# Half-array mask and memory-update matmuls, a reordered prob transpose and resets on ScalarE in a compressive-memory attention block

## What is computed

```
scores  = q @ k.T / 8, masked above the diagonal
att_dot = softmax(scores) @ v
sq, sk  = elu(q) + 1, elu(k) + 1
att_mem = (sq @ M) / (sq @ Z.T)
M, Z    = M + sk.T @ v, Z + sum(sk)          # starts again from memory0, z0 for each sequence
att     = gate * att_mem + (1 - gate) * att_dot
out     = att @ Wo
```

## Time and profile before

| | us |
|---|---|
| median of 3 runs | 1129.81 |
| lowest, highest | 1127.05, 1130.29 |
| the profiled execution, its own time | 1129.79 |
| its span from first to last instruction | 1128.0 |
| attention part (16 steps), about | from 42 to 905 in the span |
| one step in the steady state | 54.4 |

### The profile page before, as it was taken

The page is one execution under the profiler, slowest core; times in us unless marked ns, Lnnn a source line. Parts: engine busy times, 40 slices in busy tenths (PEclk is TensorE's granted clock), DMA queues, the critical chain, the costliest instruction groups (busy, mean ns, idle before and its releaser), DMA issues.

```text
span 1128.0 us, 18928 instructions
## 1 busy us (share of the span) xinstructions
PE 1026.4 (91%) x7108; PEld 726.0 (64%) x7172; DVE 779.3 (69%) x1514; ACT 617.2 (55%) x1259; POOL 561.9 (50%) x685
## 2 busy tenths in 40 slices
PE   2899999999999999899999999999998889999961
PEld 1577777776777777677777776777776755433431
DVE  4868686878778686969686968696857423434465
ACT  4556565445656464456565645565654444666562
POOL 3456565445656563547474635565654322222366
PEclk9999999999999999999999999999999889999985
DMA  5200000000000000000000000000000103000015
GB/s 159 48 11 10 14 7 16 5 20 1 20 1 20 1 20 2 19 1 20 1 20 1 20 10 10 10 11 10 1 11 1 32 0 159 1 0 0 1 38 112
DMA packets 14984, 23.82 MB, mean 21 GB/s; under 512 B 5424, under 2 KB 7216, under 8 KB 14384
## 3 DMA queue, kind: packets, MB, share of 16 engines
q1 hardware_dynamic: 13964, 19.36, 6.0%
q10 hardware_dynamic: 932, 3.28, 0.9%
HBM read 13.97 MB, written 8.65 MB: 20 GB/s over the span
## 4 chain that ended last, share of the span: by engine, by line
PE 76%; ACT 10%; DVE 8%; issue 2%; POOL 2%; DMA 1%; ACTq 0%; POOLq 0%; DVEq 0%
PE ps L1133 20%; PE ps L1230 11%; PE ps L1190 7%; PE ps L1342 7%; ACT arena L607 6%; PE ps L1177 4%; PE ps L1166 4%; PE ps L1196 4%; PE ps L1149 4%; PE ps L1355 3%; PE ps L1215 3%; PE ps L1202 3%; PE ps L1161 2%; DVE arena L855 2%; ACT arena L613 2%
## 5 line engine op out<-in xcount | busy, mean ns | idle before, releaser
L1133 PE MATMUL ps<-arena 128*128 128x512 f16 x1152 | 266.2, 381 | 6.7 <-DVE arena L807 5.2
L607 ACT ACTIVATE arena<-ps,arena 128x128 f32<-128x128 f32 x512 | 138.9, 382 | 126.7 <-DVE arena L855 126.7
L1133 PEld LDWEIGHTS ps<-arena 128*128 128x128 f16 x1152 | 112.9, 98 | 124.6 <-DVE arena L807 5.6
L830 DVE STREAM_TRANSPOSE arena<-ps 128x1024 f32<-128x1024 f32 x96 | 146.1, 1522 | 23.1 <-PE ps L1133 20.7
L436 POOL TENSOR_TENSOR arena<-arena 128x256 f32<-128x256 f32 x128 | 93.3, 729 | 136.2 <-DVE arena L874 69.5
L1190 PE MATMUL ps<-arena 128*128 128x65 f32 x1024 | 136.7, 277 | 10.3 <-ACT arena L613 4.7
L1190 PEld LDWEIGHTS ps<-arena 128*128 128x128 f32 x1024 | 128.4, 194 | 23.5 <-ACT arena L613 7.9
L421 POOL TENSOR_TENSOR arena<-arena 128x512 f32<-128x512 f32 x48 | 73.2, 1524 | 102.8 <-ACT arena L600 102.8
L782 DVE BATCH_NORM_STATS2 arena<-arena 128x6 f32<-128x256 f32 x100 | 36.9, 410 | 126.5 <-ACT arena L625 121.9
L1230 PE MATMUL ps<-arena 128*128 128x256 f32 x544 | 121.9, 382 | 0.3 <-ACT arena L619 0.3
L1230 PEld LDWEIGHTS ps<-arena 128*128 128x128 f32 x544 | 102.0, 190 | 16.1 <-ACT arena L619 1.4
(11 more groups left out here) (110 smaller groups left out, 1819.2 us busy)
## 6 DMA issues: line engine op xcount, KB each, us to landing
x_rows<-arena SPq DMA_DIRECT2D x17, 256.0 KB, 2.0
arena<-x_rows SPq DMA_DIRECT2D x4, 1024.0 KB, 7.9
out_dram<-arena SPq DMA_DIRECT2D x32, 128.0 KB, 2.9
arena<-in_L_attn_x_dram SPq DMA_DIRECT2D x62, 64.0 KB
arena<-in_L_attn_Wq_dram ACTq DMA_DIRECT2D x2, 512.0 KB, 12.2
arena<-in_L_attn_Wk_dram ACTq DMA_DIRECT2D x2, 512.0 KB, 15.2
arena<-in_L_attn_Wv_dram ACTq DMA_DIRECT2D x2, 512.0 KB, 17.8
arena<-in_L_attn_Wo_dram SPq DMA_DIRECT2D x8, 128.0 KB, 5.1
```

Of the source, the lines that this page charges most:

```text
L607: last = act.activation(Pr[:, par, j, :], s_bank[:, par, j * P:(j + 1) * P], ACT.Exp, bias=negm[:, par, j:j + 1])
L830: dve.transpose(dst[:, d0:d0 + 32], bank.rearrange("p w (d c) -> p d w c", c=C)).then_inc(x_free, 1)
L1133: last = pe.matmul(bank[:, w, :], xc[:, lx, k, w * P:(w + 1) * P], W16[lw][:, k, i, :], start=(n == 0), stop=(n == 5))
```

## The change

Six edits go together.

- **Mask.** Instead of two matmuls of 128 by 512, four: for each parity a 64-row identity (`ident2`) times `mask_top` into PSUM partitions 0 to 63 (512 columns), and times `mask_low` into partitions 64 to 127, there only the right 64 columns of each of the four blocks (256 columns). The left ones are first written by the score matmuls.
- **Update.** sk.T @ v is no longer computed in both halves of a group but only in `half == 1`, for all four `j`: eight matmuls of 128 rows by 64 output partitions and 65 columns instead of four of 128 by 130. VectorE adds it in `half == 1` alone, two adds of 64 x 260 in place of four of 64 x 130.
- **Order on TensorE.** In groups 0, 2 and 3 the turn of the next Q stands between the two parities' prob transposes, and K after them.
- **Copies of the probs.** `pt_full` counts parities, and ScalarE copies each parity's bank by itself (two of 128 x 512).
- **Resets** of M between sequence pairs: 48 VectorE copies of 64 x 130 become 24 ScalarE copies of 64 x 260, at four places of ScalarE's order, and TensorE waits for them in every segment 0.
- **Constants.** GpSimd builds only `identf` at the start, and the smaller mask and identity tiles after the low weights; TensorE waits for these before step 0.

```diff
@@ reset on ScalarE
-                def reset():
+                def reset(bp, s, g):
+                    if s != NSEG - 1 or bp == PAIRS - 1:
+                        return
+                    if bp >= 0:
+                        act.wait_ge(pm_full, bp * 32 + 8 * s + 2 * g + 2)
+                    for par in range(2):
+                        p = slice(64 * par, 64 * par + 64)
+                        act.activation(M[p, GP * g:GP * g + GP, par, :],
+                                       M0[p, GP * g % (H // 2):GP * g % (H // 2) + GP, :],
+                                       ACT.Copy).then_inc(m_reset, 1)
@@ take_p
-                    act.wait_ge(pt_full, bp * 16 + 4 * s + g + 1)
-                    act.activation(PT.rearrange("p h j i -> p (h j i)"), s_bank.rearrange("p h n -> p (h n)"),
-                                   ACT.Copy).then_inc(p_done, 1)
+                    for par in range(2):
+                        act.wait_ge(pt_full, bp * 32 + 8 * s + 2 * g + par + 1)
+                        last = act.activation(PT[:, par, :, :].rearrange("p j i -> p (j i)"), s_bank[:, par, :],
+                                              ACT.Copy)
+                    last.then_inc(p_done, 1)
@@ step on ScalarE
                     take_p(bp, s, 0)
+                    if s == 0 and bp > 0:
+                        reset(*before(bp, s), 3)
                     take_q(bp, s, 1)
@@ divide
-                    for par in range(2):
-                        p = slice(64 * par, 64 * par + 64)
-                        m = M[p, j:j + 2, par, :]
-                        if s < NSEG - 1:
-                            last = dve.tensor_tensor(m, T[p, :, par, :], m, ALU.add)
-                        elif bp < PAIRS - 1:
-                            last = dve.tensor_copy(m, M0[p, j0:j0 + 2, :])
+                    if half == 1 and s < NSEG - 1:
+                        new = pm_bank[:, :, 4 * DV1:6 * DV1].rearrange("p b (j e) -> p b j e", j=2)
+                        for par in range(2):
+                            p = slice(64 * par, 64 * par + 64)
+                            m = M[p, GP * g:GP * g + GP, par, :].rearrange("p (b j) e -> p b j e", b=2)
+                            last = dve.tensor_tensor(m, new[p], m, ALU.add)
                     last.then_inc(pm_free, 1)
@@ scores
-                        pe.matmul(s_bank[:, par, :], identb, maskS, start=True, stop=False)
+                        p = slice(64 * par, 64 * par + 64)
+                        pe.matmul(s_bank[0:64, par, :].rearrange("p (j i) -> p j i", j=GP), ident2[p],
+                                  mask_top[p].rearrange("p (a i) -> p a i", a=1).to_broadcast([64, GP, P]),
+                                  start=True, stop=False, skip_group_check=True)
+                    for par in range(2):
+                        p = slice(64 * par, 64 * par + 64)
+                        pe.matmul(s_bank[64:P, par, :].rearrange("p (j i) -> p j i", j=GP)[:, :, 64:P], ident2[p],
+                                  mask_low[p].rearrange("p (a i) -> p a i", a=1).to_broadcast([64, GP, 64]),
+                                  start=True, stop=False, skip_group_check=True)
@@ read_out
-                    if bp == 0 and s == 0:
-                        pe.wait_ge(m_reset, 2 * (g + 1))
+                    if s == 0:
+                        pe.wait_ge(m_reset, bp * 8 + 2 * (g + 1))
...
-                    if s < NSEG - 1:
+                    if half == 1 and s < NSEG - 1:
                         pe.wait_ge(sk_done, sk_count(bp, s, g) + 2)
-                        for a in range(2):
-                            h = GP * (g % 2) + 2 * half + a
-                            last = pe.matmul(pm_bank[:, a, 4 * DV1:6 * DV1],
-                                             sk[:, 2 * DK * (GP * (g - g % 2) + h):
-                                                2 * DK * (GP * (g - g % 2) + h + 1)], v[:, h, :, 0:DV1],
-                                             start=True, stop=True)
+                        for a in range(GP):
+                            h = GP * (g % 2) + a
+                            for par in range(2):
+                                unit = 2 * (GP * (g - g % 2) + h) + par
+                                last = pe.matmul(pm_bank[64 * par:64 * par + 64, a // 2,
+                                                         (4 + a % 2) * DV1:(5 + a % 2) * DV1],
+                                                 sk[:, DK * unit:DK * (unit + 1)], v[:, h, par, 0:DV1],
+                                                 start=True, stop=True)
@@ step on TensorE, group 2
-                    turn_probs(bp, s, 2)
-                    turn(bp, s, 3)
+                    turn_probs(bp, s, 2, 0)
+                    turn(bp, s, 3, "Q")
+                    turn_probs(bp, s, 2, 1)
+                    turn(bp, s, 3, "K")
```

More of the change, by code:

```diff
@@ L659, in step @@
                         take_q(bp, s, 0)
+                    reset(bp, s, 2)
                 act.sem_inc(p_done, 1)
                 take_q(0, -1, 0)
-                reset()
+                act.wait_ge(m_in, 64)
+                act.wait_ge(init, 1)
+                for g in range(GROUPS):
+                    reset(-1, NSEG - 1, g)
                 for bp, s in STEPS:
@@ L1167, in scores, with turn_probs @@
                                                  c[g % 2][p, j, :], start=False,
[L1168 removed]
+                                                 stop=(j == GP - 1 and n == 2), skip_group_check=True)
                     last.then_inc(s_full, 1)
[L1171 removed]
+                def turn_probs(bp, s, g, par):
                     G = 4 * s + g
[L1174 to L1177 removed]
+                    pe.wait_ge(e_done, bp * 32 + 2 * G + par + 1)
+                    for j in range(GP):
+                        last = pe.transpose(s_bank[:, par, j * P:(j + 1) * P], Pr[:, par, j, :], identf)
                     last.then_inc(pt_full, 1)
@@ L1276, in step @@
                     read_out(bp, s, 2, 1)
-                    turn_probs(bp, s, 3)
+                    turn_probs(bp, s, 3, 0)
                     if not last:
-                        turn(bp, s, 0)
+                        turn(bp, s, 0, "Q")
+                    turn_probs(bp, s, 3, 1)
+                    if not last:
+                        turn(bp, s, 0, "K")
                     read_out(bp, s, 3, 0)
```

59 lines of the change are left out of this document (29 added, 30 removed).

## The result

The changed kernel takes 1103.58 us (median of four runs, 1103.25 to 1103.98) against 1130.05 for the kernel before (1127.05 to 1130.38). The ratio is 0.977, with a 95% interval from 0.976 to 0.979. In the two profiled executions the span fell from 1128.0 to 1101.4 us, by 26.6 where 16.6 was expected.

The account below looks back on a forecast made before the run. TensorE was taken as mostly the bound, with VectorE's chains nearly full in C and D. Segments 1 and 2 -6.0, segment 0 -3.4, segment 3 -2.5, resets -4.7: -16.6 from 1129.81 gave 1113 us, range 1099 to 1124.

Parts of the forecast that it names:

- The central step: VectorE's chain to the next K sets C, so TensorE's saving there is lost: about 1.0 us of its gain.
- C: Stretch of a step between masks, 10.50 us before; VectorE busy 9.89; forecast +0.1 in segments 1 and 2.
- segments 1 and 2: Eight steps: A +0.1, B -0.45, C +0.1, D -0.5, sum -0.75 a step, -6.0 us in all.
- A: Stretch from group 0's mask to group 1's, 11.90 us before; chain through K outlasts its 0.30 slack, forecast +0.1.
- segment 3: Had no updates, so only copies leave: A +0.4, B -0.5, C -0.1, D -0.54; -2.5 us in all.
- the resets: A at three new pairs: VectorE copies and TensorE's 1.52 us wait go, 0.7 comes back; net -4.7 us.
- segment 0: The same as segments 1 and 2 without A: -0.85 x 4, so -3.4 us.
- 8 x 0.067: Update block on TensorE: eight pairs of 65-column records at 0.067 us, plus 0.25 for the mode, 0.78 us.
- The lower bound, 0.6: Update block on TensorE: smallest size, 0.6 us, if changing the array's tiling mode costs nothing.
- D: Stretch between masks, 10.60 us before; read-out 0.44 earlier, but later `take_x` limits project 5; forecast -0.5 with the mask.
- B: Stretch between masks, 21.40 us before; K limits it, `divide(1,0)` ahead of K loses its adds; forecast -0.45.
- Tiles one after the other: Rival: half-column matmuls do not overlap, update 2.05 us, total about 1190; decides from an update of 1.2; 5%.

## Why the prediction was right, and where its sizes were off

**What bounds.** The central step held: C did not get shorter (forecast +0.1, measured 0), VectorE's chain was on it without a gap, and taking 1.73 us out of that chain gave 1.0 us, up to TensorE's own limit.

**Where the surplus lies.** The profiled span fell by 10.0 us more than forecast: 4.3 in segments 1 and 2, 2.4 in segment 3, 0.8 in the very first A, 0.5 at the resets and 2.3 behind the last scores, less 0.4 in segment 0. The range was built on the sizes of the update and the mask, and these were nearly right. That the time still fell inside it is in part luck.

**The update** was mis-sized: 0.71 us instead of 0.78, 0.09 on the way in and 0.62 for the block. The term that was off is "8 x 0.067": the pairs come every 0.058, with 0.05 more behind the first. The 0.10 and 0.15 for the way in and out were right. The lower bound, 0.6, called "no cost of the mode", looks like the 0.62 of the block, but the cost of the mode is there. What D feels is another size: `divide(2,1)` waits for the last record of the update, and this one comes 0.17 us later than before, not the whole 0.3 by which TensorE's work was to grow. So `take_x` ended 0.39 later instead of 0.57, and D came out 0.18 below its forecast.

**A and C.** The chains were sized right: K is ready 0.40 us later in A (forecast 0.40) and 0.27 later in C. But in both the mask starts 0.10 us after K is ready, with the update alone and in the changed kernel. So the 0.09 on the way in is hidden in the wait for K, and the mask gives 0.19 and not 0.10: from the end of the K part to the first score matmul it is 0.63 us with the update alone, and 0.44 in the changed kernel. The sum had counted no gain of the mask at the end of A and 0.12 in C. With the update alone A is 12.01, as forecast; with the mask it is 11.82, 0.19 less.

**The mask**: 0.12 forecast, 0.10 measured where TensorE comes last; all four quarters run together. B holds two masks.

**Tiles one after the other** was a rival with a wrong price. Its condition, an update of over 1.2 us, was not reached by 64-column records even in two runs of one parity each (0.90). A row with records of half the width should have been scaled by width. The Trainium skill's rule (TensorE: Matmul & The Clock Gate, The mechanism), that weight loads overlap running matmuls only when the row group differs, is not what this trace shows: both parities' tiles use all 128 rows, and 16 loads go through in 0.55 us beside 0.69 us of matmuls. The section's other condition, that the weights go to the background buffer, leaves room for it.

**D.** The 0.44 from copies by parity was right to 0.01. It came from the copies, as the prediction had it, with or without the turn of Q between the probs; in C it had called the order worth nothing, and it was worth 0.07. Together with the update the gains in D overlap, and what is left is set by the adds: without them D is 9.64.

**Segment 3** was sized at half (-2.5, measured -4.9). The 0.54 for D was right (0.52), but I gave C only the mask's 0.1, and it fell by 0.42: `divide(1,1)` there had two VectorE copies before and has nothing now, so the K part ends 0.23 sooner (then the layer norm waits for GpSimd), and the mask gives 0.19 here too. The rule that VectorE's chain sets C in segments 0 to 2 was not carried over to segment 3, where the same chain got shorter by the copies. B fell by 0.63 for 0.5, the resets alone giving 0.49 of it and the mask alone 0.19, and A rose by 0.24 instead of 0.4: the update alone raises it by 0.43, and the mask takes the rest. The last 1 us of the 4.9 is the C of the last step, with its windows of the lower clock.

**Resets.** Forecast -1.3, -1.3 and -2.1, measured -1.43, -1.44 and -2.34, where 0.9 of the third is the lower clock behind TensorE's wait. The reasoning was right in both directions: VectorE's copies and their wait are gone, and a part came back over `exp_k`, GpSimd and `to_rows`: moving that reset behind `exp_k(0)` was worth 0.57, and leaving all resets out 0.89, where the prediction had given 0.7 for what comes back.

**Tail and clock** were not in the forecast: 2.3 us less behind the last scores, 1.6 more in one stretch. Neither belongs to the change. The 0.8 of the very first A had been left out of the sum: the update alone gives 0.36 there and the order 0.3, and the mask's 0.1 comes on top.

One slip is without effect: the "11 us either way" for an update from 0.6 to 0.9 is the width of that interval, at 36 us per us, and not the distance to each side.

## What to carry to other kernels

Where two engines are nearly full, price a change stretch by stretch on both of them, in each segment by itself: here the resets that left VectorE brought 7.4 us when tried alone, the mask 6.7 and the update 5.2, and the next 10 us lay in moving 1.7 us of layer norm a step to an engine that waits. Price a shorter piece by what its engine does at that point: the mask was worth 0.10 us where TensorE came to it without a gap, and 0.19 where it had to wait for K. An order that is worth nothing today can be worth 0.45 us a stretch when the bound moves, so judge it again after each change. And let records on different column halves alternate: side by side the block took 0.62 us, in runs 0.90.

## What the runs showed of the hardware

- Four 64x64 tiles (two of 512 and two of 256 columns) start within 10 ns of each other, and the next matmul, of 64 rows and 128 columns of the array, follows 0.34 us after them.
- fp32 weight loads of 64 columns, mean 137 ns each, and their matmuls of 65 columns follow each other every 0.058 us on one half of the columns; with two halves in use two come every 0.058 us.
- Going from full-array matmuls to tiles cost 0.09 us, ahead of the update (0.203 instead of 0.110 from record to record) and ahead of the mask (0.309 instead of 0.216).
- A VectorE add of 128x4 fp32 takes 0.164 us, also where a GpSimd add beside it ends 0.08 us after its start. Where the GpSimd add runs on for 0.52 us or more, it takes 0.54 to 0.61 and ends 0.02 us behind that one.
- VectorE's copy of 64x130 fp32 has a minimum of 209 ns, a median of 225 and a longest of 1332 ns. This is the line of the kernel before with its shortest, median and longest one; the six long ones all stand at the new pairs, each beside a GpSimd add of 128x512, and end 0.08 us behind it:

```profile
L876 DVE COPY arena<-arena x48: 209/225/1332, 216.5 to 699.2; 64x130 f32<-64x130 f32 x48
```

- A wait of TensorE of 1.5 to 1.6 us at the new pair can be followed by the lower clock: 4.45 us for twelve records that take 2.75. It happened at 7 of 15 such places in five executions, and at none of the 24 places without the wait.
